# Cross attention: maxima over the 48 product rows and scores over 50 rows, on 64-row tiles of the array

## The chip, the cores and the metric

The kernel is one program on one core of a Trainium2 chip. The metric is the device time of the whole kernel in microseconds. It was 1709.92 us, the median of three runs (1709.72 to 1713.21).

## What is computed

One decoder layer over 8 batches of 256 positions and 128 channels: a causal self-attention, a cross attention over a context of 1601 positions, a rotary self-attention and a mixture of experts. Only the cross attention matters here:

```python
q = x @ Wq + bq
kv = y @ Wkv + bkv
k, v = jnp.split(kv, 2, axis=-1)          # 16 heads of 8 channels each
attn = jnp.einsum('bhqd,bhkd->bhqk', q, k) * scale
attn = jax.nn.softmax(attn, axis=-1)
out = jnp.einsum('bhqk,bhkd->bhqd', attn, v)
return out.reshape(B, SQ, D_EMBED) @ Wo + bo
```

Here x is the layer-normed state of a batch, [256, 128], and y its context, [1601, 96].

## The kernel before

A head has 8 channels. To get fp32 accuracy from bf16 matmuls, each of q and k is split into three bf16 parts, and six products of parts (`PRODUCTS`, NP = 6) are summed by contracting over 6 x 8 = 48 rows (`NP * HD`). Two further rows, 48 and 49 (`SHIFT_ROW`), hold the negated row maximum in two bf16 parts against ones in the keys, so that the transposed scores come out of the matmul already shifted. These 50 rows of a head lie in one half of the 128 partitions: even heads in rows 0 to 63, odd heads in rows 64 to 127. `k_stack` [128, 8, 1602] holds the keys of two heads in one tile, one per half. `q_stack` [128, 16, 256] has a tile per head, with its rows in the head's own half and zeros in the other half, so that a matmul over all 128 rows yields this head alone.

The 16 heads are four groups of four. A batch is four rounds, one per group (round r works on group (r+1) mod 4), and a round is 13 steps, one for each tile of up to 128 keys. The instruction order of each engine is written out by hand. In a step PE issues:

- **scores** (L1532): for `par` 0, then 1, the two heads `par` and `par + 2`, stationary keys 128x128, moving queries 128x256, into one of three PSUM banks (5, 6, 7). Each pair waits until the exponential that last read its bank is done.
- **units** of the maxima (L1495): for one head, one half of the queries and one of four chunks of 400 keys, stationary queries and moving keys, into one of three banks (2, 3, 4), each waiting for DVE's reduction (L1296) of the unit three before it. A round needs 32 units, which belong to the next group: two or three per step, `units_of_step`. They take the heads in turn. The first two go behind the scores, the third behind the values.
- an **item** in some steps (`PREP_AT`): projections of the next batch's keys, queries and values (k, q, v), transposes (x, pv, attnT), the maxima's transpose (m) and the output projection (out). They go through bank 0, twenty per batch, as full-array or 96-row fp32 matmuls, between the second unit and the values.
- **values** (L1504) of the step before: four fp32 matmuls on 128x32 tiles, side by side, two records each.

ACT turns each pair of scores into probabilities (L1424, two per step) and evacuates the items. DVE reduces the units and finishes m and pv. POOL splits keys and queries into parts. SP sends the split parts of the next batch through DRAM (`bounce`, L203) and loads them into the stacks in two halves (L211); the first half is loaded when round 0 has issued its last scores, and the unit 0 that PE issues in step 9 of round 1 waits for it. The same is done for the query rows 48 and 49 (L1178) after each m item; the next round's first scores wait for it.

The first 20 units of batch 0 are issued within the self-attention (`early_units`, L946). The rotary stage behind the cross attention already has one line of 64-row matmuls, L1866, with `tile_position=(64 * hh, 0)`, its two heads in turn.

Of the kernel before, what the change touches and what calls it, by code (L numbers as in the profile page):

```python
# [12 lines left out]
P = 128  # L13
B, T, D = 8, 256, 128
QT = T // P
H, HD = 16, D // 16
# [7 lines left out]
NP = len(PRODUCTS)  # L24
TWO_ONES = 1.0019378662109375
SHIFT_ROW = NP * HD
# [148 lines left out]
def queries_of(qst, h, cols):  # L175
    return qst[:, h, cols]


def keys_of(kst, h, cols):
    return kst[:, h // 2, cols]  # L180


def stack_rows(stack, which, i, row, count, tiles):
# [167 lines left out]
def tile_rows(kt):  # L351
    return min(P, SKV - kt * P)
# [52 lines left out]
def self_attention(nc, a, t, psum, s, tables, cross, pre, early):  # L405
# [4 lines left out]
    with ctx:  # L410
# [3 lines left out]
        def sem(name):  # L414
            return ctx.enter_context(nc.semaphore(name))

        w_nat, bqk, rows = pre.w_nat, pre.bqk, pre.rows
# [39 lines left out]
        max_full, max_done = sem("a_max_full"), sem("a_max_done")  # L457
# [370 lines left out]
        def _(pe):  # L828
            T_ = Tally(PER)
# [109 lines left out]
            def early_units(units):  # L939
                for u in units:  # L940
                    if u == 0:
                        pe.wait_ge(early.half_stacked, 4 * 16)
                    wait(pe, early.max_done, u - 1)
                    q, c, hh = u // (4 * GH), u // GH % 4, u % GH
                    lo, hi = CHUNKS[c]
                    nc.tensor.matmul(psum[:, 2 + u % 2, 0:hi - lo], queries_of(t["qst"], hh, slice(q * P, q * P + P)),  # L946
                                     keys_of(t["kst"], hh, slice(lo, hi)), start=True, stop=True).then_inc(early.max_full, 1)

            def begin():
                for kind in ("x", "qk", "v", "x", "qk"):  # L950
# [46 lines left out]
def wait(eng, sem, value):  # L997

    if not isinstance(value, int) or value > 0:
        eng.wait_ge(sem, value)  # L1000
# [7 lines left out]
def units_of_step(n):  # L1008

    head = HEAD  # L1010
    if n < M_STEP:
        lo, k = UNITS_B - head, M_STEP
        return [lo + u for u in range(n * head // k, (n + 1) * head // k)]
    k, n, total = KT - M_STEP, n - M_STEP, UNITS_B - head
    return list(range(n * total // k, (n + 1) * total // k))
# [11 lines left out]
def prep_item(r, n, first=False, last=False):  # L1027

    item = PREP_AT.get((r, n))
    if item is None or (last and (item[0] in NEXT_BATCH or item == ("m", 0))):  # L1030
        return None
    if first and item[0] in ("pv", "attnT", "out"):
        return None
    return item
# [7 lines left out]
def units_left(r, n, last):  # L1042

    return not (last and (r == 2 or (r == 1 and n >= M_STEP)))
# [30 lines left out]
def cross_attention(nc, a, t, psum, s, pre, tables, early):  # L1075
# [6 lines left out]
    with ctx:  # L1082
# [3 lines left out]
        def sem(name):  # L1086
            return ctx.enter_context(nc.semaphore(name))

        wq, wo, wkv, bq, bk, rows, ctxT = pre.wq, pre.wo, pre.wkv, pre.bq, pre.bk, pre.rows, pre.ctxT
# [12 lines left out]
        qst, kst, ident = t["qst"], t["kst"], t["ident"]  # L1102
# [3 lines left out]
        def max_bank(n):  # L1106
            return psum[:, MAX_BANKS[(n - 1) % 3], :]

        def st_bank(step, par):
            return psum[:, ST_BANKS[(2 * (step - 1) + par) % 3], :]  # L1110
# [9 lines left out]
        max_full, max_done, mneg_ready = early.max_full, early.max_done, sem("b_mneg_ready")  # L1120
# [319 lines left out]
        def _(pe):  # L1440
            T_ = Tally(PER)
# [47 lines left out]
            def unit(g, u):  # L1489
                T_.up("unit")  # L1490
                wait(pe, max_done, T_.now("unit", 3))
                q, c, hh = u // (4 * GH), u // GH % 4, u % GH
                lo, hi = CHUNKS[c]
                h = g * GH + hh
                nc.tensor.matmul(max_bank(T_.now("unit"))[:, 0:hi - lo], queries_of(qst, h, slice(q * P, q * P + P)),  # L1495
                                 keys_of(kst, h, slice(lo, hi)), start=True, stop=True).then_inc(max_full, 1)

            def values():
                g, kt, buf, back = pending.pop()
# [9 lines left out]
            def prologue():  # L1509
                for name, by in (("ctx", 16), ("batch", 1), ("unit", early.N_UNITS)):  # L1510
                    T_.up(name, by)
                for u in range(early.N_UNITS, UNITS_B):
                    unit(0, u)
                item("m", 0)
                for u in range(UNITS_B - HEAD):
                    unit(1, u)

            def part(i, r, first, last):
                g = (r + 1) % 4
                for n in range(KT):  # L1520
                    T_.up("step")
                    if n == 0:

                        pe.wait_ge(m_stacked, T_.up("m_stacked", 64))

                    step = T_.now("step")
                    k, buf = tile_rows(n), (step - 1) % 2
                    for par in range(2):
                        wait(pe, exp_done, 2 * step - 1 + par - 3)
                        for hh in (par, par + 2):  # L1530
                            h = g * GH + hh
                            lastmm = nc.tensor.matmul(st_bank(step, par)[0:k, (hh // 2) * T:(hh // 2) * T + T],  # L1532
                                                      keys_of(kst, h, slice(n * P, n * P + k)),
                                                      queries_of(qst, h, slice(0, T)), start=True, stop=True)
                        lastmm.then_inc(st_full, 1)
                    units = units_of_step(n) if units_left(r, n, last) else []
                    for u in units[:1]:
                        unit_group = (g + 1) % 4 if n < M_STEP else (g + 2) % 4
                        if u == 0 and unit_group % 2 == 0:

                            pe.wait_ge(stacked, T_.up("stacked", 4 * 16))
                        unit(unit_group, u)
                    if n == 1 and not first:

                        pe.wait_ge(pv_copied, T_.now("group", -1))
                    if n == 1 and r == 3:

                        pe.wait_ge(v_placed, T_.up("placed", 2 if first else 1))
                    if n == 1 and r == 1:

                        pe.wait_ge(v_placed, T_.now("placed"))
                    for u in units[1:2]:
                        unit(unit_group, u)
                    it = prep_item(r, n, first, last)
                    if it:
                        item(*it)
                    if pending:
                        values()
                    pending.append((g, n, buf, 1))
                    for u in units[2:]:  # L1560
                        unit(unit_group, u)
                if r == 3 and not first:
                    T_.up("placed")

            parts_of_program(pe, T_, prologue, part)
            pending[0] = pending[0][:3] + (0,)
            values()
# [642 lines left out]
```

## Time and profile before

| | us |
|---|---|
| median of three runs | 1709.92 |
| the profiled execution | 1708.21 |
| its span, first to last instruction | 1706.4 |
| cross attention in it, first scores to the last | 323.6 to 1055.8 |
| one batch of it, of seven alike | 93.2 |
| PE / DVE / ACT / POOL busy over the span | 1517.9 / 1119.9 / 917.8 / 563.4 |
| mean granted clock of TensorE | 0.960 |

PE is the matmul engine, PEld its weight loads, DVE the vector, ACT the scalar, POOL the GpSimd engine, SPq the queue from which DMAs are issued. Busy shares are of the span. The record of a matmul includes its way through the array, so records overlap, and the pace of a row of matmuls is read from the distance of their starts. fp32 matmuls have two records each. A timeline row merges instructions of one line that follow each other, from the start of the first to the end of the last, and shows the count.

### The profile page before, as it was taken

To read this page: it belongs to the slowest core of one execution; us is meant where nothing else is said; L and a number is where in the kernel's file an instruction comes from. 1 tells how busy PE (TensorE), PEld (TensorE's weight loads), DVE (VectorE), ACT (ScalarE), POOL (GpSimd) and SP (SyncE) were. 2 spreads that over 40 slices of the span, in tenths; PEclk is the share of its full clock that TensorE was granted. 3 is DMA by queue.
4 is the path that set the end of the run, shared out by engine and by line. 5 is a ranking of instruction groups with operands and counts; after the bars stand their busy time and mean duration, and the time that the engine had idled before them with its cause. 6 is when DMAs were issued, how large, how long until landed. Compare 5 with 4: busy or idle time off the path is not lost. (4 is left out here: it accounts for less than half of the span.)

```text
span 1706.4 us, 29542 instructions
## 1 busy us (share of the span) xinstructions
PE 1517.9 (89%) x10917; PEld 828.5 (49%) x10941; DVE 1119.9 (66%) x2531; ACT 917.8 (54%) x1996; POOL 563.4 (33%) x695
## 2 busy tenths in 40 slices
PE   1667768899999999999999998899999999899998
PEld 1334434344444444444444443566666676544443
DVE  4855543878788787878787883566666655465554
ACT  1233325376777677777777776355555555333443
POOL 4210013030303012030303000688888788133331
PEclk9988879799999999999999999899999999899999
DMA  4232225223122323242232210000000000000001
GB/s 97 63 70 43 57 56 126 54 87 53 71 51 43 102 50 102 49 102 50 88 52 73 49 27 4 10 1 1 1 1 1 2 1 1 4 21 22 20 20 34
DMA packets 76978, 75.04 MB, mean 44 GB/s; under 512 B 12196, under 2 KB 66340, under 8 KB 75940
## 3 DMA queue, kind: packets, MB, share of 16 engines
q1 hardware_dynamic: 76836, 73.16, 19.0%
q8 instruction: 87, 1.43, 0.4%
q14 instruction: 55, 0.45, 0.1%
HBM read 42.47 MB, written 30.16 MB: 43 GB/s over the span
## 5 line engine op out<-in xcount | busy, mean ns | idle before, releaser
L1296 DVE TENSOR_REDUCE b_chunk_max<-psum 128x1 f32<-128x400 f32 x1004 | 530.6, 569 | 140.8 <-PE psum L1495 133.7
L1424 ACT ACTIVATE b_prob<-psum 128x512 f32<-128x512 f32 (+1 forms) x832 | 450.5, 594 | 182.1 <-PE psum L1532 176.2
L1495 PE MATMUL psum<-k_stack,q_stack 128*128 128x400 bf16 x1004 | 276.7, 340 | 10.1 <-DMA k_stack<-b_k_scratch 4.9
L1504 PE MATMUL psum<-b_prob,b_v_aug 128*32 128x256 f32 (+1 forms) x3328 | 265.8, 391 | 1.7 <-ACT b_prob L1424 0.4
L1532 PE MATMUL psum<-q_stack,k_stack 128*128 128x256 bf16 (+1 forms) x1664 | 254.1, 275 | 3.7 <-ACT b_prob L1424 3.3
L1532 PEld LDWEIGHTS psum<-q_stack,k_stack 128*128 128x128 bf16 (+1 forms) x1664 | 145.8, 99 | 123.0 <-ACT b_prob L1424 75.7
L1691 POOL TENSOR_SCALAR c_prob<-c_prob,c_rec 128x128 f32<-128x128 f32 (+1 forms) x256 | 192.3, 770 | 9.7 <-POOL c_kT L1700 8.6
L2106 DVE TENSOR_TENSOR e_hg<-e_gl,e_gate 128x512 f32<-128x512 f32 x124 | 122.9, 1013 | 89.0 <-PE psum L2154 84.4
L1774 DVE SCALAR_TENSOR_TENSOR c_turned<-psum,c_bias,c_tab 128x256 f32<-128x256 f32 x256 | 106.1, 476 | 112.7 <-PE psum L1907 112.7
L1809 ACT ACTIVATE c_prob<-psum,c_mneg 128x128 f32<-128x128 f32 (+1 forms) x256 | 104.1, 418 | 137.6 <-DVE c_mneg L1751 137.6
L2046 ACT ACTIVATE e_gl<-psum,b1T 128x512 f32<-128x512 f32 x124 | 85.2, 687 | 127.6 <-PE psum L2149 125.9
L1495 PEld LDWEIGHTS psum<-k_stack,q_stack 128*128 128x128 bf16 x1004 | 97.6, 98 | 112.8 <-DVE b_chunk_max L1296 89.8
L1907 PE MATMUL psum<-c_xT,c_w 128*128 128x256 f32 x512 | 130.0, 400 | 1.9 <-DVE c_turned L1774 1.5
L2154 PE MATMUL psum<-e_hg,e_w 128*128 128x512 f32 x248 | 126.1, 592 | 0.7 <-DVE e_hg L2106 0.7
L2149 PE MATMUL psum<-anT,e_w 128*128 128x512 f32 x248 | 126.6, 592 | 0.0
L400 POOL COPY b_v_aug<-b_v_new 128x768 f32<-128x768 f32 (+1 forms) x32 | 15.9, 529 | 335.0 <-issue 251.0
L1504 PEld LDWEIGHTS psum<-b_prob,b_v_aug 128*32 128x32 f32 (+1 forms) x3328 | 65.7, 108 | 124.4 <-issue 94.3
L2022 POOL PARTITION_BROADCAST e_gate<-e_gate_row x30 | 69.9, 2331 | 125.3 <-DMA e_gate_row<-gatesT 122.9
L698 DVE TENSOR_REDUCE a_mneg<-psum 128x2 f32<-128x512 f32 (+1 forms) x96 | 65.4, 689 | 62.9 <-PE psum L910 62.0
L1907 PEld LDWEIGHTS psum<-c_xT,c_w 128*128 128x128 f32 x512 | 98.1, 202 | 15.5 <-DVE c_turned L1774 2.6
L809 ACT ACTIVATE a_prob<-psum 128x1024 f32<-128x1024 f32 x64 | 51.9, 810 | 67.1 <-PE psum L881 65.1
L2154 PEld LDWEIGHTS psum<-e_hg,e_w 128*128 128x128 f32 x248 | 47.0, 190 | 60.3 <-issue 58.6
(236 smaller groups left out, 1950.7 us busy)
## 6 DMA issues: line engine op xcount, KB each, us to landing
k_stack<-b_k_scratch SPq DMA_DIRECT2D x32, 600.4 KB, 10.2
b_k_scratch<-b_kparts SPq DMA_DIRECT2D x7, 1200.8 KB, 4.4
b_k_scratch<-b_kparts SPq DMA_DIRECT2D x7, 800.5 KB, 6.1
b_ctxT<-in_ctx SPq DMA_DIRECT2D x8, 600.4 KB, 11.8
e_w<-in_L_ffn_re_w SPq DMA_DIRECT2D x62, 64.0 KB, 1.9
a_scratch<-a_parts SPq DMA_DIRECT2D x16, 192.0 KB, 2.1
q_stack<-b_q_scratch SPq DMA_DIRECT2D x32, 96.0 KB, 2.2
b_k_scratch<-b_kparts SPq DMA_DIRECT2D x7, 400.2 KB, 6.7
```

The lines of the kernel that those rows point to most:

```text
L1296: nc.vector.tensor_reduce(out=chunk_max[:, half, q, column4(hh), c:c + 1], in_=max_bank(v)[:, 0:w], axis=AX.X, op=ALU.max).then_inc(max_do ...
L1424: nc.scalar.activation(prob[0:k, buf, par * 2 * T:(par + 1) * 2 * T], st_bank(v, par)[0:k, :], ACT.Exp, scale=HD ** -0.5).then_inc(exp_don ...
L1495: nc.tensor.matmul(max_bank(T_.now("unit"))[:, 0:hi - lo], queries_of(qst, h, slice(q * P, q * P + P)), keys_of(kst, h, slice(lo, hi)), st ...
L1504: last = nc.tensor.matmul(pv[32 * hh:32 * hh + 32, :], v_aug[0:k, kt, g * GH + hh, :], prob[0:k, buf, c:c + T], start=(kt == 0), stop=(kt ...
L1532: lastmm = nc.tensor.matmul(st_bank(step, par)[0:k, (hh // 2) * T:(hh // 2) * T + T], keys_of(kst, h, slice(n * P, n * P + k)), queries_of ...
L1691: ins = nc.gpsimd.tensor_scalar(prob[:, w % PB, hh, lo:hi], prob[:, w % PB, hh, lo:hi], rec[:, w % PB, hh, q:q + 1], None, ALU.mult)
L1774: ins = nc.vector.scalar_tensor_tensor(out=turned[:, u % 2, m, w, :], in0=bank[:, w * T:(w + 1) * T], scalar=bias[:, m, w, u:u + 1], in1=t ...
L1809: ins = nc.scalar.activation(prob[:, u % PB, hh, lo:hi], psum[:, 2 + hh, lo:hi], ACT.Exp, bias=mneg[:, par, q, hh:hh + 1], accum_out=total ...
L1907: last = nc.tensor.matmul(bank[:, w * T:(w + 1) * T], weights[:, m, u * P:(u + 1) * P], xT[:], start=True, stop=True)
L2106: nc.vector.tensor_tensor(hg[:, c, :], gl[:, c, :], gate[e % 2][:, cols(c)], ALU.mult).then_inc(hg_ready, 1)
L2149: nc.tensor.matmul(psum[:, 4 + c, :], w[:, (e + 1) % 3, 0, :], d["anT"][:, cols(c)], start=True, stop=True)\
L2154: nc.tensor.matmul(psum[:, c, :], w[:, (e + 1) % 3, 1, :], hg[:, c, :], start=False, stop=False).then_inc(y_done, 1)
```

## The change

The maxima (both places) now contract over 48 rows and the scores over 50, each in the half of the rows where the head lies, and each matmul is placed on a tile of 64 rows of the array: `tile_position` (0, 0) for even heads, (64, 0) for odd ones. The zeros of the other half of `q_stack` are still written, and no longer read by these lines. The two heads of one score pair have the same half; the pairs of a step have different halves, and the units alternate. Banks, the order of the instructions and all waits are as before.

```diff
+def rows_of(h, count):
+    return slice(64 * (h % 2), 64 * (h % 2) + count)
...
-                    nc.tensor.matmul(psum[:, 2 + u % 2, 0:hi - lo], queries_of(t["qst"], hh, slice(q * P, q * P + P)),
-                                     keys_of(t["kst"], hh, slice(lo, hi)), start=True, stop=True).then_inc(early.max_full, 1)
+                    rows = rows_of(hh, NP * HD)
+                    nc.tensor.matmul(psum[:, 2 + u % 2, 0:hi - lo], t["qst"][rows, hh, q * P:q * P + P], t["kst"][rows, hh // 2, lo:hi],
+                                     start=True, stop=True, tile_position=(rows.start, 0)).then_inc(early.max_full, 1)
...
-                nc.tensor.matmul(max_bank(T_.now("unit"))[:, 0:hi - lo], queries_of(qst, h, slice(q * P, q * P + P)),
-                                 keys_of(kst, h, slice(lo, hi)), start=True, stop=True).then_inc(max_full, 1)
+                rows = rows_of(h, NP * HD)
+                nc.tensor.matmul(max_bank(T_.now("unit"))[:, 0:hi - lo], qst[rows, h, q * P:q * P + P], kst[rows, h // 2, lo:hi],
+                                 start=True, stop=True, tile_position=(rows.start, 0)).then_inc(max_full, 1)
...
+                            rows = rows_of(h, SHIFT_ROW + 2)
                             lastmm = nc.tensor.matmul(st_bank(step, par)[0:k, (hh // 2) * T:(hh // 2) * T + T],
-                                                      keys_of(kst, h, slice(n * P, n * P + k)),
-                                                      queries_of(qst, h, slice(0, T)), start=True, stop=True)
+                                                      kst[rows, h // 2, n * P:n * P + k], qst[rows, h, :],
+                                                      start=True, stop=True, tile_position=(rows.start, 0))
```

## Rows read from the trace of the kernel before

**Rows 1.** The page: busy time, share of the span and instructions of each engine.

```profile
PE 1517.9 (89%) x10917; PEld 828.5 (49%) x10941; DVE 1119.9 (66%) x2531; ACT 917.8 (54%) x1996; POOL 563.4 (33%) x695
```

**Rows 2.** Windows: length, busy PE, PEld, DVE, ACT, POOL, clock, DMA, GB/s.

```profile
439.05:462.10 23.05, 21.72 (x179) 10.31 (x178) 18.01 (x40) 17.37 (x34) 12.32 (x13) 1.00 0.01 2
462.10:483.24 21.14, 20.57 (x189) 11.39 (x189) 14.32 (x29) 14.70 (x29) 3.89 (x7) 1.00 0.79 203
483.24:489.69 6.45, 6.25 (x59) 2.71 (x58) 5.88 (x13) 4.70 (x9) 0.00 (x0) 1.00 0.00 1
489.69:510.37 20.68, 20.48 (x193) 9.64 (x192) 17.71 (x37) 14.82 (x28) 0.00 (x0) 1.00 0.01 3
510.37:532.24 21.87, 21.31 (x199) 10.45 (x198) 18.63 (x40) 15.21 (x29) 1.00 (x2) 1.00 0.54 94
```

**Rows 3.** Groups by line, cross attention, 340 to 1040 us: count, busy, mean, idle.

```profile
L1296 DVE TENSOR_REDUCE b_chunk_max<-psum 128x1 f32<-128x400 f32 (+1 forms) x958 | 507.2, 570 | 137.1 <-PE psum L1495 130.2
...
L1495 PE MATMUL psum<-k_stack,q_stack 128*128 128x400 bf16 (+1 forms) x958 | 259.6, 335 | 8.4 <-DMA k_stack<-b_k_scratch 4.9 <-DVE b_chunk_max L1296 2.5
...
L1532 PE MATMUL psum<-q_stack,k_stack 128*128 128x256 bf16 (+1 forms) x1569 | 239.0, 274 | 3.3 <-ACT b_prob L1424 3.3
L1532 PEld LDWEIGHTS psum<-q_stack,k_stack 128*128 128x128 bf16 (+1 forms) x1568 | 137.5, 99 | 113.2 <-ACT b_prob L1424 68.3 <-issue 24.3
```

**Rows 4.** Timeline of steps with three units: start, duration, engine, line, count.

```profile
600.05 5.91 DVE L1296 TENSOR_REDUCE b_chunk_max<-psum 128x1 f32<-128x400 f32 x11 [0.47 <-PE psum L1495]
...
600.87 0.60 PE L1532 MATMUL psum<-q_stack,k_stack 128*128 128x256 bf16 x4
...
601.30 0.50 PE L1495 MATMUL psum<-k_stack,q_stack 128*128 128x400 bf16 x2
...
601.74 0.64 PE L1504 MATMUL psum<-b_prob,b_v_aug 128*32 128x256 f32 x8
...
602.31 0.34 PE L1495 MATMUL psum<-k_stack,q_stack 128*128 128x400 bf16 x1
...
602.49 0.60 PE L1532 MATMUL psum<-q_stack,k_stack 128*65 128x256 bf16 x4
```

**Rows 5.** Timeline of a step with two units, from score to score.

```profile
1002.44 0.61 PE L1532 MATMUL psum<-q_stack,k_stack 128*128 128x256 bf16 x4
...
1002.93 1.09 ACT L1424 ACTIVATE b_prob<-psum 128x512 f32<-128x512 f32 x2
...
1003.89 0.61 PE L1532 MATMUL psum<-q_stack,k_stack 128*128 128x256 bf16 x4
```

**Rows 6.** Timeline of PE in the rotary stage, around its 64-row matmuls.

```profile
1201.53 1.89 PE L1907 MATMUL psum<-c_xT,c_w 128*128 128x256 f32 x8
...
1203.57 0.93 PE L1866 MATMUL psum<-c_kT,c_qT 64*128 64x128 f32 x8
1204.43 0.39 PE L1869 MATMUL psum<-mask_qk,identb 128*128 128x256 bf16 x2
```

**Rows 7.** Timeline of the chain from the query item to the next first maximum.

```profile
462.10 0.59 PE L1458 MATMUL psum<-b_xT,b_wq 128*128 128x256 f32 x2
...
465.31 0.67 POOL L1231 TENSOR_TENSOR b_qparts<-b_qrest,b_qparts 128x256 bf16<-128x256 f32 x1
...
471.99 0.93 SPq L211 DMA_DIRECT2D k_stack<-b_k_scratch  x2
...
483.24 0.50 PE L1495 MATMUL psum<-k_stack,q_stack 128*128 128x400 bf16 x2
```

**Rows 8.** Issues to landing, waits and one stall: the k_stack transfer, cross attention.

```profile
k_stack<-b_k_scratch SPq DMA_DIRECT2D x28, 600.4 KB, 8.8
...
671.62 0.51 PE L1495 MATMUL psum<-k_stack,q_stack 128*128 128x400 bf16 x2 [1.30 <-DMA k_stack<-b_k_scratch]
```

**Rows 9.** Windows: the granted clock in self-attention, columns as before.

```profile
100.00:200.00 100.00, 73.54 (x602) 44.02 (x616) 54.30 (x155) 32.85 (x60) 9.62 (x16) 0.83 0.22 49
...
305.30:325.80 20.50, 17.01 (x47) 6.00 (x48) 17.11 (x36) 1.86 (x5) 0.00 (x0) 0.50 0.36 91
```

## The prediction

> **What bounds the kernel now.** I read the page first. PE is busy 89% of the span, more than any other engine [rows 1]. One batch cut at its four rounds then shows that PE is busy 90.3 us of 93.2, DVE 74.6, ACT 66.8 [rows 2]. So PE sets the pace here, but DVE idles only 18.6 us per batch, and this is all that a faster PE can win before DVE takes over. The sum of that stage is in the groups of lines: 958 maxima, 1569 scores and DVE idle 137 us ahead of its reductions, 130 of it waiting for L1495 [rows 3].
>
> Next come two steps of the timeline. I call the four score matmuls of a step S (A0, A2 are the heads of the lower row half, B1, B3 of the upper), a maximum U and the values block V. S is 0.60 us for four, with 0.27 us the life of one [rows 3, 4], so they start (0.60-0.27)/3 = 0.109 us apart; two U take 0.50, one 0.335, so they start 0.167 apart. From the start of V to the next block is 0.57 us (601.74 to 602.31), and from the last U's start (601.47) to V 0.27, which is 0.17 of streaming and 0.10 of gap [rows 4]. A step with three units lasts 602.49-600.87 = 1.62 us, one with two 1003.89-1002.44 = 1.45 [rows 4, 5]. A round has 13 steps, 6 with three units and 7 with two (the split of 21 units over 9 steps and 11 over 4).
>
> DVE reduces 11 units in 5.91 us, 0.537 each [rows 4]. Three make 1.61 us: **the three-unit steps already run at DVE's pace**, and only the two-unit steps (DVE 1.07, ACT 1.09 [rows 5], PE 1.45) and the steps with an item leave something to win.
>
> **The change, part by part.** (1) Contracting over 48 or 50 rows instead of 128 changes no matmul's own time: columns stay 256 and 400. The rotary stage has 64-row matmuls to compare with [rows 6]: eight records of L1866, two row halves in turn, four of 128 and four of 256 fp32 columns. L1907 gives 256 fp32 columns one after another, (1.89-0.38)/7 = 0.216 us apart, so 0.108 for 128. One by one the eight would last 4x0.108+3x0.216+0.38 = 1.46 us; as pairs, with one exposed weight load of about 0.1, 2x0.108+0.216+0.38+0.1 = 0.91. The row shows 0.93. **Different row halves run side by side.**
>
> (2) In a step S is ordered A0 A2 B1 B3 and units alternate halves. The lower half streams A0, A2 and one U: 2x0.109+0.167 = 0.385. The upper half may start when A2 has started, 0.109 later: 0.109+2x0.109+0.167 = 0.494. Now it is 4x0.109+2x0.167 = 0.770. So S and two U save 0.276 us on PE, and a step becomes 0.494+0.10+0.57 = 1.16 us with two units, 1.33 with three, 1.17 where the third unit (behind V) is of the upper half and the next A0 runs beside it. A cost is possible that the trace doesn't show for bf16 with 64 rows: a weight load no longer hidden. Bounds: from nothing (the loads of [rows 4] keep the matmuls' 0.109, hidden) to the fp32 load's 0.1 per block. I take nothing, as bf16 of the same 128 columns is the nearest row; the other end stays in the range.
>
> (3) Switching tile shape. Going from 128x128 to 64x128 or back costs what any change of shape costs in the rows: L1866's last start plus its stream to L1869 is about 0.09 us (1203.57+0.93-0.38+0.21 = 1204.33, to 1204.43) [rows 6], U to V 0.10 [rows 4]. Before, U and the items (128x128) shared a shape and only V differed; now S and U share one, so each of a batch's 20 items adds one switch: 20x0.095 = 1.9 us of PE per batch. The Trainium skill ("TensorEngine Tiling (Array Packing)", Key Properties) says that changing the tiling mode drains the TensorE, which speaks against this change; the trace agrees, with the 0.09 to 0.10 above, and without that drain the sum would be 13 us larger. The same skill ("TensorE: Matmul & The Clock Gate", Part 3) has weight loads overlap running matmuls only where the row groups differ. Here four full-array bf16 loads of 99 ns [rows 3] and their matmuls start 0.109 apart, which is streaming alone, so in this trace the rule doesn't hold. By the rule each of a step's six loads would stand open for its 0.099, 0.6 us that a two-unit step of 1.45 us has no room for, and the change would gain by it; the sum goes by the row.
>
> (4) Where the gain lands, by stretch of a batch [rows 2]:
> - **Round 0 to the query item** (23.05 us, DVE idle 5.0). Eleven steps gain 0.276 on PE, 3.0; two or three third units run beside the next A0, 0.3; seven items cost 0.7. That is 2.6, but in steps 0 to 2 and 9 to 10 DVE (two 1 us normalisations, units, the negated maximum) is next late. I take 2.3.
> - **Query item to the next batch's first maximum** (21.14 us). Here a chain runs that PE doesn't shorten: query matmul 462.10, ACT, POOL's last split 465.31+0.67, three bounces, the two k_stack loads issued from 471.99 on, first U of unit 0 at 483.24 [rows 7], and those loads take 8.8 us in median to land [rows 8]. In four of the seven batches PE already waits there for the k_stack transfer, 4.9 us in all [rows 3], 1.30 in one [rows 8]. DMA is at 0.79 busy in this stretch [rows 2]. So eleven of a batch's 52 steps gain nothing: 0.1 us.
> - **The rest of round 1** (6.45): DVE has 9 of 11 units in three-unit steps; only its idle 0.57 can go. I take 0.45.
> - **Round 2** (20.68, DVE idle 2.97): three times two steps of two units and one of three, now 4.52 us, become DVE-bound at 7x0.537 = 3.76, since PE needs 2x1.16+1.33 = 3.65. That is 2.3; the gap after the m item adds 0.4; PE's margin of 0.1 in 3.7 will not feed DVE without gaps, and two items cost 0.2. I take 2.0.
> - **Round 3** (21.87, DVE idle 3.24): the same with four items and more of DVE's own work. 2.0.
>
> Together 6.9 us per batch, seven batches 48. Outside: the round ahead of them (323.6 to 344.5) 1.9, the last batch's round 0 2.0, ten steps of its round 1 1.3, the tail 0.3, because without units a step is 0.44+0.67 = 1.11 against ACT's 1.09. The 20 early units of the self-attention go at DVE's pace: nothing. Sum 54 us of the 656 and its ends. The profiled execution took 1708.2 us (1706.4 of span and 1.8 around it), 1.7 below the median of 1709.9, so its own sum is 1654; taken from the median, **1656 us**.
>
> **The rivals.** (A) *The halves overlap only in part*: a same-half neighbour (A0 A2, B1 B3), a load that is not hidden, or the wait ahead of B1 blocks the queue, so S and U save half, 0.14. For: in L1866 the halves alternate, in S they don't. Against: in the same rows two matmuls of one half follow each other at streaming pace, so the queue does run ahead. PE keeps the pace: 41 steps x 8 x 0.14 less the switches, about 30 us, 1680.
> (B) *Slower: no overlap, only switches.* If bf16 halves stream one after another, nothing is saved and the 20 items per batch pay 0.095 on PE, which has no slack: 7x1.9 = 13, less the part hidden in the chain stretch, 1709.9+11 = 1721 us. It decides from the point where a batch's overlap gains less than 1.9 us, that is 0.036 us for each of its 52 steps. Against it stands the L1866 row.
> (C) *Slower: the clock falls.* With fewer busy columns PE's granted clock could go to 1.2 GHz for parts of the stage. It was 0.83 over a stretch of self-attention with PE busy 0.74, and 0.50 from 305.3 to 325.8 with PE busy 17.0 of 20.5; in all five stretches of cross attention it is 1.00 [rows 2, 9]. After the change PE is still streaming for 0.97 of a two-unit step's 1.16 us and about 1.1 of a DVE-paced step's 1.61, and its gaps stay below 1 us. At the self-attention's 0.83 a third of 400 steps would stream at half speed, about 1.0 us more each: 1656+137 = 1790 us.
> (D) *DVE and PE interlock better than I take it*: all of DVE's idle outside the chain goes, 5.0+0.6+3.0+3.2 = 11.8 per batch, 83 with 7 outside, 1620 us. Some gaps (the normalisation's own waits) are not PE's, so I cap it near 1632.
> (E) *No change*: gains and switches cancel, or another chain, such as the store of the two maximum rows that the next round's S waits for, holds the rounds. Against: it has steps 10 to 12 to land, nine units of DVE, 4.83 us, before and after the change.
>
> **How the numbers follow.** Chances: forecast (1640 to 1672) 0.58, D below it 0.07, A 0.18, E 0.05, B 0.08, C 0.04. The likeliest is the forecast, 1656. The range leaves out C, B, E and the outer part of D: 1636 to 1698. A measurement of this kernel can tell 0.2%, 3.4 us: faster 0.83, same 0.05, slower 0.12.
>
> **What the next profile would show.** Right: S of four lasting 0.50 instead of 0.60; two-unit steps near 1.16 to 1.25; DVE idle before its reductions down from 137 us to below 90; the wait of L1495 for k_stack up from 4.9 us to 15 or more; the batch near 86 us; the clock 1.00 through the stage. Item steps gain less than plain ones by 0.1. Wrong: S still at 0.60 (B), a load idle between A2 and B1 (A), the clock below 1.00 (C). The prediction fails most likely in how well DVE is fed, which I took from sums, not from an order of events.

## The result, and the profile after

The kernel after took 1704.04 us, the median of 18 runs (1688.04 to 1716.56); the kernel before, beside it, 1708.71 (1704.9 to 1713.21). The ratio is 0.9944, with a 95% interval of 0.992 to 0.9968; it is that of the means, without the four slowest runs of after (1714.03 us and more), which count as slow, and with all 18 it is 0.9966. So the change gained 0.3 to 0.6%. The forecast of 1656 was 48 us too low, and the time lies outside the range of 1636 to 1698. The spread has grown too: 28.5 us between the fastest and the slowest run, where before has 8.3. The fastest run has a mean granted clock of 0.931, the slowest 0.906. The profiled execution took 1711.87 us, of which 1710.0 is span, at a mean clock of 0.910; that of before had 0.960.

The page of after, to be read against [rows 1], with the row of TensorE's granted clock in 40 slices of the span:

```profile
PE 1490.1 (87%) x10917; PEld 734.6 (43%) x10941; DVE 1105.1 (65%) x2531; ACT 914.7 (53%) x1996; POOL 563.7 (33%) x695
...
PEclk9978879689898897999688999899999999899999
```

PE is busy 28 us less, and it still is the busiest engine, although the change was to save 54 us. The cross attention fills slices 9 to 25. In the windows [rows 2] of before the clock stood at 1.00, and here eight of those slices show only 6 to 8 tenths. The next views say where.

Windows of one batch of after, cut at the first scores of each round (columns as in [rows 2]); then two parts of its round 0, and the round 0 of another batch:

```profile
441.67:473.60 31.93, 30.05 (x218) 10.41 (x215) 20.87 (x46) 20.58 (x41) 13.78 (x16) 0.73 0.07 28
473.60:497.90 24.30, 20.61 (x215) 8.63 (x211) 16.72 (x35) 15.96 (x32) 2.44 (x5) 0.93 0.60 141
497.90:516.11 18.21, 17.41 (x197) 6.33 (x194) 17.14 (x38) 15.00 (x29) 0.00 (x0) 1.00 0.01 3
516.11:536.14 20.03, 18.41 (x204) 7.06 (x201) 18.00 (x41) 15.04 (x30) 1.00 (x2) 1.00 0.58 103
441.67:448.90 7.23, 6.40 (x57) 2.23 (x53) 6.97 (x18) 5.33 (x12) 3.59 (x4) 1.00 0.01 2
448.90:465.90 17.00, 16.54 (x90) 4.80 (x92) 7.63 (x17) 9.06 (x17) 7.69 (x8) 0.50 0.00 0
725.18:750.62 25.44, 23.50 (x218) 9.11 (x215) 20.74 (x46) 20.26 (x41) 13.79 (x16) 1.00 0.10 37
```

Rounds 2 and 3 (third and fourth row) came as forecast: 18.21 and 20.03 where [rows 2] has 20.68 and 21.87, at clock 1.00, with DVE busy 17.14 of 18.21. Round 0 did not: 31.93 us, because from 448.90 on PE worked for 17 us at half its clock, 1.2 GHz of 2.4, busy 16.54 of 17.00. DVE and ACT then wait for PE. In the batch from 725.18 the clock stayed at 1.00, and the same round took 25.44. So the time splits like this (us, first scores to first scores; all seven full batches of a run):

| round | before | after, each batch | after less before, summed |
|---|---|---|---|
| 0 | 26.83 | 31.77, 31.93, 33.33, 30.54, 25.44, 35.59, 31.85 | +32.6 |
| 1 | 23.8 to 25.2 | 25.79, 24.31, 22.54, 26.34, 25.45, 28.10, 24.08 | +5.8 |
| 2 | 20.68 | 18.12 to 18.34 | -17.5 |
| 3 | 21.88 | 20.02 | -13.0 |
| the round ahead, and the last batch | | | -4.1 |

The sum is +3.8 us, and the two profiled executions differ by 3.7. The time at half clock within the cross attention is 165.3 us, against 2.2 us in before: 111.0 in rounds 0, 42.1 in rounds 1 (18.7 of it the tail of a fall of round 0), 0.5 in a round 2 and 11.7 in the round ahead of the first batch, where the 2.2 of before are too. Round 0 alone lost 220.5-7x25.44 = 42 us to it. The falls of round 0 begin 7 to 10 us behind its first score, in steps 3 and 4. The batch from 725.18 has the same first 7.23 us (PE busy 6.39 us for 6.40) and no fall, so the fall is not certain there. The last batch, whose round 0 prepares no next batch, has none.

The groups by line, 340 to 1040 us, as [rows 3]:

```profile
L1302 DVE TENSOR_REDUCE b_chunk_max<-psum 128x1 f32<-128x401 f32 x960 | 492.0, 567 | 154.6 <-PE psum L1502 147.4
...
L1502 PE MATMUL psum<-k_stack,q_stack 48*128 48x400 bf16 (+1 forms) x959 | 261.2, 361 | 32.1 <-DMA k_stack<-b_k_scratch 17.5 <-DVE b_chunk_max L1302 8.5 <-ACT b_pvs L1416 0.2
L1540 PE MATMUL psum<-q_stack,k_stack 50*128 50x256 bf16 (+1 forms) x1557 | 200.4, 291 | 3.6 <-ACT b_prob L1430 3.6
```

PE's waits for the keys' transfer rose from 4.9 to 17.5 us, so it is early where it runs at full clock. DVE's idle ahead of its reductions did not fall from 137.1 but rose to 154.6: it sums well-fed rounds 2 and 3 with starved rounds 0.

The steps themselves, in the timeline of PE at full clock (start, duration, engine, line):

```profile
413.12 0.40 PE L1540 MATMUL psum<-q_stack,k_stack 50*128 50x256 bf16 x4
413.35 0.34 PE L1502 MATMUL psum<-k_stack,q_stack 48*128 48x401 bf16 x2
413.62 0.64 PE L1511 MATMUL psum<-b_prob,b_v_aug 128*32 128x256 f32 x8
414.19 0.46 PE L1540 MATMUL psum<-q_stack,k_stack 50*128 50x256 bf16 x4
```

Four scores last 0.40 us, two units 0.34 (both start together), and the step 414.19-413.12 = 1.07 us, where [rows 5] has 1.45. That is the shortest step of a round: it is PE's own work without a wait, and already as short as the 1.09 of ACT's two exponentials in [rows 5] and the 1.07 of DVE's two reductions. The other five two-unit steps of a round 2 are 1.23 to 1.47 us, as DVE, busy 17.14 of its 18.21 us, now sets the pace there.

And the chain to the keys of the next batch, in the undisturbed batch, from the query item to the first unit that needs the transfer (as [rows 7]):

```profile
747.04 0.70 PE L1464 MATMUL psum<-b_xT,b_wq 128*128 128x256 f32 x2
...
768.60 0.34 PE L1502 MATMUL psum<-k_stack,q_stack 48*128 48x400 bf16 x2 [2.56 <-DMA k_stack<-b_k_scratch]
```

It lasts 21.56 us, where [rows 7] has 21.14. Over the batches, to the landing, it is 20.4 to 22.8 before and 20.8 to 23.05 after.

### The profile page after: what moved, and what is told of

Read it like the earlier page. It is cut to its first block and busy times, and to the rows that moved or that the text cites. A ratio compares the mean times of both kernels' runs of the same rounds, so it can differ in the third digit from the quotient of the medians.

```text
span 1710.0 us, 29542 instructions
## 1 busy us (share of the span) xinstructions
PE 1490.1 (87%) x10917; PEld 734.6 (43%) x10941; DVE 1105.1 (65%) x2531; ACT 914.7 (53%) x1996; POOL 563.7 (33%) x695
## 5 line engine op out<-in xcount | busy, mean ns | idle before, releaser
L1302 DVE TENSOR_REDUCE b_chunk_max<-psum 128x1 f32<-128x400 f32 x1004 | 514.0, 567 | 159.5 <-PE psum L1502 152.1
L1502 PE MATMUL psum<-k_stack,q_stack 48*128 48x400 bf16 x1004 | 277.7, 367 | 34.3 <-DMA k_stack<-b_k_scratch 17.5
L1511 PE MATMUL psum<-b_prob,b_v_aug 128*32 128x256 f32 (+1 forms) x3328 | 293.0, 427 | 2.4 <-ACT b_pvs L1416 0.4
L1540 PE MATMUL psum<-q_stack,k_stack 50*128 50x256 bf16 (+1 forms) x1664 | 215.1, 292 | 4.2 <-ACT b_prob L1430 3.6
L1502 PEld LDWEIGHTS psum<-k_stack,q_stack 48*128 48x128 bf16 x1004 | 84.6, 100 | 188.5 <-DVE b_chunk_max L1302 112.3
L1540 PEld LDWEIGHTS psum<-q_stack,k_stack 50*128 50x128 bf16 (+1 forms) x1664 | 75.0, 98 | 118.2 <-issue 58.6
```

The lines of the kernel that those rows point to most:

```text
L1302: nc.vector.tensor_reduce(out=chunk_max[:, half, q, column4(hh), c:c + 1], in_=max_bank(v)[:, 0:w], axis=AX.X, op=ALU.max).then_inc(max_do ...
L1502: nc.tensor.matmul(max_bank(T_.now("unit"))[:, 0:hi - lo], qst[rows, h, q * P:q * P + P], kst[rows, h // 2, lo:hi], start=True, stop=True, ...
L1511: last = nc.tensor.matmul(pv[32 * hh:32 * hh + 32, :], v_aug[0:k, kt, g * GH + hh, :], prob[0:k, buf, c:c + T], start=(kt == 0), stop=(kt ...
```

## The experiments

The theory after this view was: the overlap works, and the halves take TensorE's clock away in rounds 0 and 1, because a matmul on 64 rows counts as less than a full one. The rivals were: the clock falls because PE has short gaps or shorter busy times as such; or because the data changed (zeros no longer streamed); or the loss is a wait, with the clock only following it. Scores, units, items and values are named as in the kernel's description.

**The same kernel again (r_after).** No edit.

> The changed kernel once more, beside the others on one chip. Its 18 timed runs spread from 1688 to 1717 us with a mean granted clock from 0.931 down to 0.906, and its profile has 165 us of cross attention at half clock, all in rounds 0 and 1 of the batches. If the clock is what ate the gain, the time of each run goes with its clock here too: about 1.1 us per 0.001. If it is not, time and clock are unrelated.

It took 1705.43 us (ten runs, 1683.84 to 1711.66) beside 1707.83; the ratio is 0.9949 [0.9916, 0.9983]. Half-clock time in the cross attention was 141.6 us, 11.5 of it in a round 2, where a fall that began in round 1 went on. Run by run the time goes with the mean clock, 1683.8 at 0.931 and 1711.7 at 0.914, about 1.4 us per 0.001 over the ten, where 1.1 was expected. The loss is a property of the kernel, and its size varies from run to run.

**All heads in the lower half (e1).** Every matmul of the scores and maxima is a half-row one, and none has another half beside it.

```diff
-    return slice(64 * (h % 2), 64 * (h % 2) + count)
+    return slice(0, count)
```

> The changed kernel with the maxima and scores of odd heads also taken from rows 0 to 63 (which hold zeros for them), so that no two matmuls lie in different halves; the output of odd heads is meaningless. Rows theory (the clock falls because half-row matmuls leave half of the array idle): nothing overlaps, PE streams as long per step as before the change, and still the clock falls at least as often as after the change, above 165 us at half clock in cross attention, 1730 us or more. Idle theory (the clock falls because faster scores and maxima leave PE waiting): the steps last 1.45 and 1.62 us again, the clock stays at 1.00 in cross attention, and the time is that of before plus the item switches, 1709 + 11 = 1720 us.

It took 2281.33 us, ratio 1.3356 [1.3329, 1.3383]. If the halves' overlap alone were lost, the step would be that of before or little more, near 1721 us (rival B). Instead the clock was at half when the stage began and never rose in it, 1300 us of 1300. The window, 656 us of cross attention:

```profile
347.00:1003.00 656.00, 655.40 (x3194) 247.20 (x3191) 297.25 (x611) 264.56 (x504) 68.65 (x88) 0.50 0.18 39
```

and a step in the timeline of PE, in which no gap shows:

```profile
459.43 0.87 PE L1502 MATMUL psum<-k_stack,q_stack 48*128 48x400 bf16 x2
460.23 1.08 PE L1511 MATMUL psum<-b_prob,b_v_aug 128*32 128x256 f32 x8
461.25 1.03 PE L1540 MATMUL psum<-q_stack,k_stack 50*128 50x256 bf16 x4
462.07 0.87 PE L1502 MATMUL psum<-k_stack,q_stack 48*128 48x400 bf16 x2
```

PE is busy 655.40 of 656.00 us at clock 0.50. **Gaps can't be what holds the clock down here, there are hardly any.** The idle theory had asked for a clock of 1.00 and 1720 us, the rows theory for 1730 us or more, and only the second survives: "busy" in the profile is not what keeps the clock up.

**The same with real data (e1b).** In the run before, odd heads read zeros, which could be the cause. Here they read the query tile of their even neighbour, so that all rows carry numbers.

```diff
-                nc.tensor.matmul(..., qst[rows, h, q * P:q * P + P], kst[rows, h // 2, lo:hi],
+                nc.tensor.matmul(..., qst[rows, h - h % 2, q * P:q * P + P], kst[rows, h // 2, lo:hi],
```

> As e1_lower, which stayed at half clock through all of cross attention (2281 us), but the odd heads now read the query tile of their even neighbour, so that rows 0 to 49 hold real data for all heads and no zeros; the output of odd heads is meaningless. Rows theory: half of the array idle is what keeps the clock down, so the clock is 0.50 through cross attention again and the time within 1% of 2281 us. Data theory (the clock follows how much the operands switch, and e1_lower fed zeros for half of the heads): the clock recovers in part, the time is well below, 2000 us or less.

One run, 2283.26 us:

```profile
347.00:1003.00 656.00, 655.40 (x3191) 247.09 (x3189) 297.32 (x611) 264.86 (x505) 68.64 (x88) 0.50 0.18 39
```

It is the same as with zeros, so zeros in the operands are not what holds the clock down in e1.

**Full rows, equally short (e2b).** The kernel before, its scores cut to 128 of 256 query columns; ACT reads each written half twice. PE is relieved nearly as much as by the change (scores and two units 0.55 us for 0.50), with all 128 rows in use.

```diff
-    nc.tensor.matmul(st_bank(step, par)[0:k, (hh // 2) * T:(hh // 2) * T + T], ..., queries_of(qst, h, slice(0, T)), ...)
+    nc.tensor.matmul(st_bank(step, par)[0:k, (hh // 2) * T:(hh // 2) * T + P], ..., queries_of(qst, h, slice(0, P)), ...)
```

> The kernel before, full rows, with each score matmul cut to 128 of its 256 query columns (ACT reads each written half of a head's part twice, its own time unchanged); queries 128 to 255 are left out of the scores. S shortens from 0.436 to 0.218 us, S and two units from 0.77 to 0.55, near the changed kernel's 0.50, with all rows of the array in use. Rows theory: the clock stays at 1.00, rounds 2 and 3 last about 18.3 and 20.2 us, round 0 about 25.5, the time is 1655 to 1662 us. Idle theory: the clock falls in rounds 0 and 1 as after the change, above 100 us at half clock, 1695 us or more.

It took 1667.31 us (1664.61 to 1670.01), ratio 0.9761 [0.9738, 0.9784]. The first 7.23 us of a round 0 (to be read against the 7.23 us ahead of a fall, above), the whole round 0, and round 2 of one batch:

```profile
431.13:438.36 7.23, 6.15 (x54) 2.63 (x52) 6.97 (x17) 5.62 (x12) 3.58 (x4) 1.00 0.01 2
431.13:456.16 25.03, 23.02 (x213) 10.53 (x212) 20.43 (x45) 20.22 (x41) 13.96 (x16) 1.00 0.10 38
...
481.13:499.51 18.38, 17.96 (x193) 7.71 (x192) 17.12 (x37) 14.66 (x29) 0.00 (x0) 1.00 0.01 3
```

PE is busy 23.02 of 25.03 us in round 0, 0.92, which is the share of after's undisturbed round 0 (23.50 of 25.44), and in no batch does the clock fall there, although PE is less busy in the first 7.23 us than in after (6.15 for 6.40). **With no less idle time, it is the half rows that make the clock fall in round 0.** But in six of the seven rounds 1 the clock fell here too, five times for 3.4 us and once for 6.8, right behind PE's wait for the keys, which lasted 2.2 to 3.7 us; behind the seventh wait, 1.7 us, it didn't. In after the falls behind this wait are 3.4 us three times and 6.8 twice. So the falls of round 1 need no half rows, only a PE that comes early to this wait. Half-clock time is 26 us in all, where after has 165. With a PE that is fast enough and nearly keeps its clock, the kernel takes what I had forecast within 12 us.

**Half rows in rounds 2 and 3 only (e4).** A rule decides per step; where it is false, the matmul uses `slice(0, P)`, all rows, as before. The third unit, which stands behind the values, takes the shape of the next step.

```diff
+def halves(r, n):
+    return r in (2, 3)
...
-                            rows = rows_of(h, SHIFT_ROW + 2)
+                            rows = rows_of(h, SHIFT_ROW + 2) if halves(r, n) else slice(0, P)
```

> The changed kernel with 64-row tiles only in rounds 2 and 3 (where its profile has the full clock), full rows in rounds 0 and 1. Both theories: no falls of the clock beyond before's; round 2 lasts 18.1 instead of 20.7, round 3 20.0 instead of 21.9, rounds 0 and 1 as before: 4.4 us per batch, 31 in all and 2 at the ends, 1675 us, ratio 0.980. If the falls come from anything earlier than the half-row work itself (a state carried over from round 3), they stay in rounds 0 and 1 and the time is above 1690.

It took 1676.98 us (1674.31 to 1678.49), ratio 0.9816 [0.9801, 0.9831], for an expected 1675. Rounds 0, 2 and 3 of a batch:

```profile
435.25:462.08 26.83, 25.51 (x214) 12.62 (x213) 20.78 (x45) 20.56 (x40) 14.29 (x16) 1.00 0.11 45
...
485.72:503.85 18.13, 17.28 (x198) 6.34 (x195) 16.97 (x37) 14.60 (x29) 0.00 (x0) 1.00 0.01 3
503.85:524.05 20.20, 18.57 (x203) 7.17 (x200) 18.17 (x41) 15.15 (x30) 1.00 (x2) 1.00 0.59 102
```

The gain of rounds 2 and 3 stays, round 0 is that of before, and half-clock time is 11.5 us, all in the round ahead of the first batch. That is 9 us more than in before, which neither theory had expected: this round works with half rows too, begins at half clock, and with full rows the clock is up after 2.2 us (before and e2b). Using half the change makes the kernel 27 us faster than all of it: the loss sits in rounds 0 and 1. It also speaks against a state carried over from round 3.

**Half rows in more of the dense steps (e5).** Steps 4 to 10 of round 0 and the last batch are added (`halves` from here on takes the batch `i` and `last` as well).

```diff
-    return r in (2, 3)
+    return last or r in (2, 3) or (r == 0 and 4 <= n <= 10)
```

> e4_r23 and more: 64-row tiles in rounds 2 and 3, in steps 4 to 10 of round 0, and in the whole last batch. Falls of the clock begin in steps 2 to 4 of round 0 after the change, where PE waits for DVE and an item. If only that sparse start trips the clock, steps 4 to 10 gain about 1.0 us per batch (k_stack lands about 22 us behind the query item whatever PE does, so all that is gained ahead of the query item stays) and the last batch 4.6: 1677 - 7 - 3 = 1667 us. If seven steps of half-row work behind the sparse start trip it as well, round 0 lasts 28 to 30 us in some batches and the time is 1680 or more.

It took 1667.67 us (1664.48 to 1671.3), ratio 0.9775 [0.9748, 0.9803]: **2.25% below before and below the kernel after**, for an expected 1667. The interval holds 0.98, so that it gains 2% is not certain. One batch, its four rounds:

```profile
432.54:458.31 25.77, 24.18 (x213) 10.65 (x212) 20.64 (x45) 20.27 (x40) 14.30 (x16) 1.00 0.11 43
458.31:481.95 23.64, 22.98 (x212) 11.69 (x211) 17.36 (x36) 16.12 (x31) 1.94 (x5) 1.00 0.61 136
481.95:500.07 18.12, 17.28 (x197) 6.32 (x193) 16.96 (x37) 14.61 (x29) 0.00 (x0) 1.00 0.01 3
500.07:520.28 20.21, 18.58 (x204) 7.17 (x201) 18.19 (x41) 15.17 (x30) 1.00 (x2) 1.00 0.60 102
```

All at 1.00, as in all seven batches; half-clock time is 14.9 us, 11.5 of it ahead of the first batch and one fall of 3.4 in the last. Half rows that have the other half beside them, in steps that begin at full clock, don't cost the clock in themselves; it depends on where they stand.

**Half rows everywhere but at the start of round 0 (e9).** This asks whether the falls of round 0 start in its first four steps, where DVE has the two normalisations and PE waits for it.

```diff
+    return last or not (r == 0 and n < 4)
```

> 64-row tiles everywhere except in steps 0 to 3 of round 0 of each batch but the last. Rows theory: the falls of round 0 go; those of round 1, which follow the wait for k_stack, stay, each 3 to 7 us at half clock, as after the full change. Round 0 about 25.8 us, rounds 2 and 3 18.1 and 20.0, time 1665 to 1675 us. If the round 0 falls need no sparse start, they stay, 1690 or more.

It took 1676.51 us (1673.46 to 1679.56), ratio 0.982 [0.9782, 0.9858], just above what was expected. Round 0 is 25.26 us, without any fall: four steps of thirteen, given back to full rows, save 6 us a round. But round 1 is 24.36 to 26.31, with 3.4 to 9.5 us at half clock in each. The 9.5 are the start of one long fall: it goes on for 17.8 us of a round 2, whose dense half-row steps kept the clock at 1.00 in the other batches (but for a rest of 0.3 us) and didn't bring it back up in this one. PE's longest waits there (time, times, longest):

```profile
PE psum L1507 <- DMA k_stack<-b_k_scratch: 21.4, 7, 3.9
```

All seven batches now wait for the keys, 3.1 us each in the mean, and the clock falls behind that wait: 3.4 us five times, once 6.8 and once 27.3. The full rows of e2b have the same 3.4 us behind the same wait, so only the long fall is more than theirs.

**The same, with a short load (e10).** The steady loads of `k_stack` bring 400 of 1601 keys. The rest of the keys is stale, so the result means nothing; the order of work is the same.

```diff
-                load_stack(sp, (qst, kst)[which], (q_scr, k_scr)[which], which, slice(4 * half, 4 * half + 4), done)
+                load_stack(sp, (qst, kst)[which], (q_scr, k_scr[:, :, 0:400])[which], which, slice(4 * half, 4 * half + 4), done)
```

> e9_r0start with the k_stack loads of the steady batches cut to the first 400 of 1601 keys (the other keys keep what the first batch left; the output is meaningless). Chain theory (round 1 can't shrink because its step 9 waits for k_stack, about 22 us behind the query item, and the clock's falls in round 1 follow that wait): the wait goes, round 1 lasts 20 to 21 us instead of 24.4 to 26.3, no falls in rounds 1 and 2, the time is 1676 less 7 x 4.6 = 1644 us. If round 1 is bound by its own items, it stays above 22.5 us and the time above 1658.

It took 1644.72 us (1644.17 to 1645.27), ratio 0.9628 [0.9601, 0.9655], where 1644 was expected. Round 1 of a batch:

```profile
457.65:478.85 21.20, 19.64 (x216) 8.47 (x213) 16.65 (x36) 16.18 (x32) 2.42 (x5) 1.00 0.35 119
```

No wait for the keys, no fall in rounds 1 and 2, and round 1 at 21.20 instead of 24 to 26. So in e9 the chain to `k_stack` costs 3 to 5 us in round 1 of each batch, part as waiting and part as lost clock behind it.

**As e5, with half rows at the ends of rounds 0 and 1 as well (e11).** The steps from 9 of round 1 on lie behind the unit that waits.

```diff
+    return last or r in (2, 3) or (r == 0 and 4 <= n) or (r == 1 and n >= M_STEP)
```

> e5_more (1668 us) with 64-row tiles also in steps 11 and 12 of round 0 and 9 to 12 of round 1. Without more falls of the clock: the query item comes 0.2 us earlier and DVE's first gap behind the wait closes, 0.3: 1664 us. Rows theory warns that step 9 of round 1 stands right behind the longest idle stretch of PE: if half-row work there keeps the clock down or drops it, rounds 1 and 2 lengthen by 2 to 6 us in some batches and the time is 1670 or more.

It took 1668.95 us (1663.73 to 1671.6), ratio 0.9764 [0.9734, 0.9793]: not to be told from the 1667.67 above, and 5 us over the 1664 that it was to take without more falls. In three of seven batches the clock fell in round 1 (3.4, 8.4 and 3.4 us), and the fall of 8.4 went on for 8.7 us of round 2. The longest such round:

```profile
722.98:750.30 27.32, 25.03 (x212) 11.29 (x211) 17.69 (x36) 16.22 (x31) 2.27 (x5) 0.85 0.53 124
```

What the half rows win (a batch without a fall is 86.8 to 88.4 us, for 87.7 to 88.9 in e5), the falls give back. Whether the half rows behind the wait bring them is not shown, as the wait is longer too: 1.7 to 2.1 us in the three batches that fell (and 2.1 in one that didn't), 1.0 to 1.4 in e5.

**Scores alone (e6), and maxima alone (e7)**, both in rounds 2 and 3. These ask what a change of tile shape costs, since between scores and units there now is one more.

```diff
# e6, in all three places that issue a unit
-                        unit(unit_group, u, halves(i, r, n, last))
+                        unit(unit_group, u)
# e7
-                            rows = rows_of(h, SHIFT_ROW + 2) if halves(i, r, n, last) else slice(0, P)
+                            rows = slice(0, P)
```

> 64-row tiles for the scores alone, in rounds 2 and 3 alone; the maxima use full rows everywhere. By the prediction's prices S gains 0.109 us by its one overlapping pair and pays 0.095 for the switch to the full-array units, and in three-unit steps another 0.095 for the switch from the third unit to the next S: two-unit steps 1.44, three-unit steps 1.70, round 2 about 21.2 us against 20.7 before. If a switch costs nothing, round 2 lasts 19.3 to 19.8.

> 64-row tiles for the maxima alone, in rounds 2 and 3 alone. e6_scores showed the four scores of a step in 0.40 us, both halves from the start (0.218 of streaming instead of 0.436), and a two-unit step of 1.35. If a pair of units overlaps as fully (0.167 for two) and each added switch costs 0.095: two-unit steps 1.45 - 0.167 + 0.095 = 1.38, three-unit steps 1.62 - 0.167 + 0.19 = 1.64; round 2 about 20.2 us. If the units don't overlap, 21.5.

The first took 1700.53 us, the second 1711.95, one run each. Scores alone, then maxima alone, in the timeline of PE from score to score:

```profile
500.38 0.40 PE L1545 MATMUL psum<-q_stack,k_stack 50*128 50x256 bf16 x4
500.71 0.51 PE L1507 MATMUL psum<-k_stack,q_stack 128*128 128x400 bf16 x2
501.16 0.64 PE L1516 MATMUL psum<-b_prob,b_v_aug 128*32 128x256 f32 x8
501.73 0.40 PE L1545 MATMUL psum<-q_stack,k_stack 50*128 50x256 bf16 x4
```

```profile
500.12 0.61 PE L1545 MATMUL psum<-q_stack,k_stack 128*128 128x256 bf16 x4
500.66 0.34 PE L1507 MATMUL psum<-k_stack,q_stack 48*128 48x400 bf16 x2
500.93 0.64 PE L1516 MATMUL psum<-b_prob,b_v_aug 128*32 128x256 f32 x8
501.50 0.61 PE L1545 MATMUL psum<-q_stack,k_stack 128*128 128x256 bf16 x4
```

A two-unit step is 1.35 us with half-row scores alone and 1.38 with half-row units alone, for 1.45 in [rows 5]. The scores end streaming after two pairs, 2x0.109 = 0.22; the first unit starts 0.33 behind the first score, so the switch is 0.11 us. With maxima alone the units start 0.54 behind, of which 4x0.109 = 0.44 is streaming: 0.10. **The price of 0.095 per switch holds.** The rounds missed their expectations in opposite ways: round 2 took 19.99 for scores alone (21.2 expected, as the overlap of the scores is complete and not half) and 20.74 for maxima alone (20.2 expected). With maxima alone the three-unit steps rise to 1.66 us, from 1.62, and the item step 2 of round 2 from 1.85 to 2.03, which takes back what two-unit steps win. So the 2.5 us that round 2 gained need both parts: each alone pays a switch per step and brings 0.7 and -0.1.

These two runs also bear on a rival that no run was made for, that the clock falls because of the switches of tile shape and not of the rows. Both have more switches per step than e4 and kept 1.00 in rounds 2 and 3. And in the round ahead of the first batch the clock stayed at half for 1.4 us with half-row maxima, 4.7 with half-row scores and 11.5 with both (e4): it goes with the amount of half-row work, not with the switches. In round 0, where most falls are, the two were not separated.

## Why the prediction was wrong, by its own steps

- **(1) Halves side by side**: right. Both units start together. In e1, which has no other half to run beside, four scores take 1.03 us at half clock, with starts 0.21 apart, one after another.
- **(2) S and two U from 0.770 to 0.494**: right in kind, and the gain was larger. I had B1 wait until A2 has started; it starts beside A0 (last section). Four scores last 0.40 instead of the 0.50 named, so they stream in two pairs, 0.22 and not 0.33, and from the first score to V it is 413.62-413.12 = 0.50 with the 0.10 switch in it, for 0.59. The shortest two-unit step is 1.07, for 1.16 forecast; most are longer and go at DVE's pace. No load stood open.
- **(3) The switch**: right, 0.10 and 0.11 for 0.095.
- **(4) Where it lands**, at full clock: rounds 2 and 3 gained 2.5 and 1.85 us for 2.0 each. Round 0 to the query item gained 23.05-21.86 = 1.2 for 2.3; that DVE's normalisations and the units behind them hold its first steps is argued, as DVE is busy 6.97 of the first 7.23 us. The chain of 21 us stayed, as forecast, and round 1 gained nothing measurable, for 0.55. No batch of after has the full clock in all four rounds, so I put one together from its rounds: 25.44+24.3+18.12+20.02 = 87.9 us, for 86.3 forecast (the 24.3 holds one fall of 3.4 us). Seven of these are 615 us, where the batches of before are 656.5; with the 4.1 us of the ends the kernel would take about 1665 us by this estimate, inside the range. This part was off by 9 us, by the terms of rounds 0 and 1.
- **(C) The clock**: this step failed, and the other 39 of the 48 us are its. The sum put the clock at no cost, and I gave the rival 0.04 because PE would still be busy and its gaps would stay below 1 us. Two things were wrong with that. First, it takes PE's busy share for what keeps the clock; e1 refutes it, with PE busy 655.40 of 656.00 us at 0.50. Half-row matmuls that have the other half beside them kept 1.00 in rounds 2 and 3 where these rounds began with it; half-row matmuls in the first steps of round 0 lost it, and full-row ones with no less idle time didn't (e2b). Second, the gaps did not stay below 1 us, and my own list of signs had 15 us or more of waits for the keys in seven batches, 2 us each. They were 1.8 to 4.1 us in six batches, and most such waits were followed by a fall, as they were with full rows (e2b). The hint was in the trace of before: in [rows 9] PE is busy 17.01 of 20.50 us at 0.50, so a high busy share didn't keep the clock there either. The size of the rival, 137 us for a third of the steps at half clock, was too high: the falls took 165 of the stage's 736 us, and cost 42 us in round 0, where they can be told from the rest.
- The Trainium skill ("TensorE: Matmul & The Clock Gate", Part 1) has the clock follow how busy PE has been of late. The busy time that the profile prints doesn't decide it here, as the row of e1 shows.
- **What the profile would show**: of the signs of being right, the wait for the keys (17.5 us, "15 or more") came true, and the scores (0.40, "0.50") and the shortest two-unit step (1.07, "1.16 to 1.25") went beyond it; DVE's idle (154.6, "below 90") and the batch (89.3 to 101.8 us, "86") did not; and the sign of (C), "the clock below 1.00", did.

**What stays open.** Why a fall lasts 3.4 us in one batch and 44 in another; what the chip counts exactly, rows in use, their number over time, or power; and why the same kernel had 141.6 and 165.3 us at half clock in two profiles. For round 0 the runs show the cause by exclusion (half rows in its first steps; not idle time, not data) and the place, not the rule. For round 1 they show falls behind a wait of about 2 us or more with either shape; why a few of them last 17 to 27 us, and only with half rows, is open. A cure for round 1, starting the chain to `k_stack` earlier, was not tried; the run with the short load, 1644.7 us, is 23 us below e5 and suggests what it could bring.

## What to carry to other kernels

Tiles of 64 rows do run side by side and can halve the time of thin matmuls, but a stretch in which they leave PE room can fall to half clock, and then the gain is gone. Pair every half with the other one; half-row work without it stayed at half clock throughout (e1). Use the tiles where PE sets the pace and the stretch is dense, and leave full rows in steps in which PE waits for another engine. A PE made faster also comes earlier to a wait for a DMA, and the clock can fall behind that wait whatever the rows, so shorten the wait itself. And read the granted clock stretch by stretch rather than PE's busy share. A rival about the clock wants a chance that the profile supports, and "the gaps are short" doesn't make it small, the less so where the forecast itself lengthens a wait.

## What the runs showed of the hardware

- **PE can be busy all the time and stay at 1.2 GHz**, here for the whole 656 us of the window (e1 and e1b), at 1.34 times the kernel's time. Halves in pairs don't always bring the clock back either: in r_after PE was busy all of 17.1 us from 955.2 on, at 0.50, at the end of round 1 and in round 2.
- **Four matmuls ordered A0 A2 B1 B3 run as two pairs.** Their starts in after are two within 7 ns and two more 0.12 us later, and the first of the units stands 0.23 behind the first score. The records don't name the head, but in the program only the second matmul of each pair, A2 and B3, increments a semaphore. In the packed trace the two records at 413.121 and 413.127 carry no increment, and those at 413.241 and 413.247 do. So B1 starts beside A0 and ahead of A2, out of program order. It is so in 250 of the 416 steps of after, and in none of the 416 of before or e2b. The Trainium skill ("TensorE: Matmul & The Clock Gate", Part 3) has matmuls start strictly in program order; these records don't agree with it.
- **A wait can cost the clock behind it, with full rows too**: behind waits of 2.2 to 3.7 us for a DMA the clock fell for 3.4 us five times and for 6.8 once (e2b, full rows), and behind waits of 2.3 to 3.9 us for 3.4 us five times, once for 6.8 and once for 27.3 (e9, half rows). Behind waits of 1.7 us or less with full rows it didn't fall (before, e2b, e4, e5).
